# Two dense attentions with exponentials over three score banks, two score places and a ring of 15 units

## What is computed

```python
x = x + L0_attn(ln(x)); x = x + L0_ffn(ln(x))
x = x + L1_attn(ln(x)); x = x + L1_ffn(ln(x))
x = x + L2_attn(ln(x)); x = x + L2_ffn(ln(x))      # L2_attn: dense softmax attention + a sparse one
x = x + L3_attn(ln(x)); x = x + L3_ffn(ln(x))      # L3_attn: dense softmax attention
# the dense attention, 16 heads of 8 channels, 2048 tokens
scores = einsum('bhqd,bhkd->bhqk', q, k) * scale
out    = einsum('bhqk,bhkd->bhqd', softmax(scores), v)
```

## Time and profile before

| | us |
|---|---|
| median of 3 runs | 3074.58 (3073.29 to 3082.42) |
| the profiled execution, its own time | 3076.39 |
| its span, first to last instruction | 3074.5 |
| ACT in L1770, third layer / fourth layer | 495.7 / 496.0 |
| PE in L1729, third / fourth layer | 275.6 / 268.4 |
| PE in L1743, third / fourth layer | 274.2 / 268.4 |
| first dense attention, first half (in the trace) | 1486 to 1739 |
| first dense attention, second half | 1845 to 2109 |
| second dense attention | 2495 to 2998 |

### The profile page before, as it was taken

The page is one execution under the profiler, slowest core; times in us unless marked ns, Lnnn a source line. Parts: engine busy times, 40 slices in busy tenths (PEclk is TensorE's granted clock), DMA queues, the critical chain, the costliest instruction groups (busy, mean ns, idle before and its releaser), DMA issues. The chain is left out here.

```text
span 3074.5 us, 33207 instructions
## 1 busy us (share of the span) xinstructions
PE 2411.5 (78%) x12588; PEld 839.1 (27%) x12588; DVE 1912.1 (62%) x2779; ACT 1996.6 (65%) x1976; POOL 1072.1 (35%) x404
## 2 busy tenths in 40 slices
PE   3567777766757676765999889998669759999995
PEld 1122222244222222332222232223434412222223
DVE  5777988857999999866888527995330510111115
ACT  4789999912733333242899758997331259999991
POOL 4889999811099999431001200022000000000000
PEclk8888999979888888887999998999879879999998
DMA  2011112110154444102201200101010130111000
GB/s 72 1 42 42 42 56 69 42 52 8 28 171 159 163 161 157 52 13 64 43 13 35 40 0 2 20 3 43 7 39 0 44 53 14 35 29 22 14 6 27
DMA packets 66891, 144.63 MB, mean 47 GB/s; under 512 B 15592, under 2 KB 29889, under 8 KB 66018
## 3 DMA queue, kind: packets, MB, share of 16 engines
q1 hardware_dynamic: 66722, 142.40, 16.4%
HBM read 117.92 MB, written 24.25 MB: 46 GB/s over the span
## 5 line engine op out<-in xcount | busy, mean ns | idle before, releaser
L601 POOL TENSOR_TENSOR l0a_diff_pool<-l0a_A,l0a_a_of_t 128x2048 f32<-128x2048 f32 x128 | 532.5, 4203 | 36.2 <-ACT l0a_a_of_t L616 36.2
L1770 ACT ACTIVATE l2x_pT<-ps 128x1024 f32<-128x1024 f32 x512 | 495.7, 1021 | 17.9 <-PE ps L1729 16.0
L1770 ACT ACTIVATE l3he_pT<-ps 128x1024 f32<-128x1024 f32 x512 | 496.0, 1021 | 4.7 <-PE ps L1729 2.8
L1182 PE MATMUL ps<-l1s_hc,all_ident 128*128 128x512 f32 x512 | 287.7, 716 | 152.8 <-POOL l1s_hc L1153 100.6
L580 DVE SCALAR_TENSOR_TENSOR l0a_diff_dve<-l0a_A,l0a_pos,ps 128x512 f32<-128x512 f32 x512 | 344.9, 742 | 44.0 <-PE ps L455 44.0
L1144 POOL TENSOR_TENSOR l1s_dBx<-l1a_dtx,l1a_Bs 128x1024 f32<-128x1024 f32 x128 | 297.7, 2356 | 109.6 <-POOLq L878 109.6
L1168 ACT ACTIVATE ps<-l1a_dt,l1a_A 128x1024 f32<-128x1024 f32 x128 | 143.0, 1118 | 268.4 <-DVE l1s_hc L1227 216.1
L1729 PE MATMUL ps<-l3h_Qs,l3h_Ks 75*128 75x512 bf16 x1024 | 268.4, 385 | 33.0 <-DVE ps L1818 33.0
L1833 DVE COPY l3he_oT<-ps 128x512 f32<-128x512 f32 x16 | 11.1, 692 | 445.7 <-PE ps L1743 445.6
L1729 PE MATMUL ps<-l2m_Qs,l2m_Ks 75*128 75x512 bf16 x1024 | 275.6, 394 | 9.8 <-PEq L2052 9.8
L1743 PE MATMUL ps<-l2x_pT,l2m_Va 128*9 128x512 f32 x2048 | 274.2, 609 | 1.2 <-ACT l2x_pT L1770 1.2
(11 more groups left out here) (420 smaller groups left out, 3350.9 us busy)
## 6 DMA issues: line engine op xcount, KB each, us to landing
l1a_Bs<-l1a_bc SPq DMA_DIRECT2D x64, 512.0 KB, 3.6
l1s_Cs<-l1a_bc SPq DMA_DIRECT2D x64, 512.0 KB, 4.7
l0a_band_rows<-l0a_band SPq DMA_DIRECT2D x32, 512.0 KB, 5.4
l0a_band<-l0a_exps SPq DMA_DIRECT2D x16, 512.0 KB, 5.1
l2m_Ks<-l2m_parts SPq DMA_DIRECT2D x36, 128.0 KB
l2m_Qs<-l2m_parts SPq DMA_DIRECT2D x72, 64.0 KB
l3h_Ks<-l3h_parts SPq DMA_DIRECT2D x36, 128.0 KB
l3h_Qs<-l3h_parts SPq DMA_DIRECT2D x72, 64.0 KB
```

What stands on the lines that cost most here:

```text
L601: pool.tensor_tensor(out, window(s), atb[:, p % 2, :].unsqueeze(1).broadcast_to([P, 4, CH]), ALU.subtract).then_inc(diff_pool, 1)
L1182: mm = pe.matmul(g.ps[:, (4 + 2 * h + q) * CH:(5 + 2 * h + q) * CH], g.ident[:, :], hc[:, m % NHC, q * CH:(q + 1) * CH], start=(n == 0), s ...
L1770: act.activation(pT[:, turn % NPT, :], g.ps[:, slot * QC:(slot + 1) * QC], ACT.Exp).then_inc(expd, 1)
```

## The change

It alters the schedule of the two dense attentions and nothing else. The unit of the ring and of the accounting becomes the score block of 512 queries.

- **Exponentials over 1536 columns.** Units are taken three at a time, in triples; one ACT instruction reads three banks and writes three units. An attention of 1024 units has 342 of them instead of 512 (the last has one unit; each of the third layer's two halves of 512 units has 171, the last with two).
- **Two places of three banks** for the scores (`NST = 2`): triple `t` may be written when exponential `t - 2` is done.
- **A ring of 15 units** (`NPT = 15`) instead of 8 turns, which were 16 units; the place is the unit modulo 15.
- **Order on PE.** After each triple's scores at most one (n, c) of values is issued, if its last unit lies in triple `t - 2` or before; what is left at the end follows behind.
- **Waits on ACT.** Each triple waits for its scores, and for the values (of each half `c` that occurs) that read the units 15 earlier.
- SP's waits at a segment's end ask for the triple that holds the segment's last unit.

```diff
-NPT, NST = 8, 3
-ACC = NST * QC
+NPT, NST = 15, 2
+WIDE = 3 * CH
+ACC = NST * WIDE
...
+def triple_of(u, first):
+
+    done = 8 * TB * first
+    return -(-done // 3) + (u - done) // 3
...
 def head_values(pe, g, hd, pT, expd, accr, pvd, n, c, first):
...
-    if c == 0:
-        pe.wait_ge(expd, 4 * n + 4)
+    pe.wait_ge(expd, triple_of(8 * n + 6 + c, first) + 1)
...
 def head_segments(pe, g, hd, pT, sps, expd, accr, pvd, first, last):
 
+    due = [(n, c) for n in range(first * TB, last * TB) for c in range(2)]
+    for t, units in triples(first, last):
+        if t >= NST:
+            pe.wait_ge(expd, t - NST + 1)
+        for k, u in enumerate(units):
+            mm = head_scores(pe, g, hd, sps, u, (t % NST) * WIDE + k * CH)
+        mm.then_inc(sps, 1)
+        if due and triple_of(8 * due[0][0] + 6 + due[0][1], first) <= t - NST:
+            head_values(pe, g, hd, pT, expd, accr, pvd, *due.pop(0), first)
+    for n, c in due:
+        head_values(pe, g, hd, pT, expd, accr, pvd, n, c, first)
+
+
+def head_exps(act, g, pT, sps, expd, pvd, first, last):
+
+    for t, units in triples(first, last):
+        act.wait_ge(sps, t + 1)
         for c in range(2):
+            old = [(u - NPT) // 8 + 1 for u in units if u - NPT >= 8 * TB * first and (u - NPT) % 2 == c]
+            if old:
+                act.wait_ge(pvd[c], max(old))
+        at, src = ring_place(units[0], first), (t % NST) * WIDE
+        act.activation(pT[:, at:at + len(units), :], g.ps[:, src:src + len(units) * CH].rearrange("p (u t) -> p u t", t=CH), ACT.Exp).then_inc(expd, 1)
```

More of the change, by code:

```diff
@@ L1451 @@
 NQ = T // QC
-SEG = TB * 4
 NSEG = G4 * NQ
-NPT, NST = 8, 3
-ACC = NST * QC
+NPT, NST = 15, 2
+WIDE = 3 * CH
+ACC = NST * WIDE
 HB = TB // 2
@@ L1713, in head_prepare, with ring_place, exps_through, triples @@
     return hd
-def head_scores(pe, g, hd, pT, sps, expd, n, j):
+def triple_of(u, first):
+    done = 8 * TB * first
+    return -(-done // 3) + (u - done) // 3
+def ring_place(u, first):
+    return (u - 8 * TB * first) % NPT
+def exps_through(seg, first):
+    return triple_of(8 * TB * (seg + 1) - 1, first) + 1
+def triples(first, last):
+    units = range(8 * TB * first, 8 * TB * last)
+    return [(triple_of(units[k], first), units[k:k + 3]) for k in range(0, len(units), 3)]
+def head_scores(pe, g, hd, sps, u, at):
+    n, rest = divmod(u, 8)
+    j, c = divmod(rest, 2)
     seg, kt = divmod(n, TB)
     hg, qc = divmod(seg, NQ)
[L1720 to L1724, removed]
+    if kt == 0 and rest == 0:
         pe.wait_ge(hd.q_in[qc], hd.QIN * (hg + 1))
@@ L1727, in head_scores, with head_values @@
             pe.wait_ge(hd.k_in[hg % 2], hd.KIN * (hg // 2 + 1))
[L1728 to L1734, removed]
+    return pe.matmul(g.ps[:, at:at + CH], hd.Ks[:, hg % 2, j, kt * P:(kt + 1) * P], hd.Qs[:, qc, j, c * CH:(c + 1) * CH], start=True, stop=True)
+def head_values(pe, g, hd, pT, expd, accr, pvd, n, c, first):
     seg, kt = divmod(n, TB)
     hg = seg // NQ
-    if c == 0:
-        pe.wait_ge(expd, 4 * n + 4)
+    pe.wait_ge(expd, triple_of(8 * n + 6 + c, first) + 1)
     if kt == 0 and seg:
@@ L1743, in head_values @@
         mm = pe.matmul(g.ps[32 * j:32 * j + HS + 1, ACC + c * CH:ACC + (c + 1) * CH],
-                       hd.Va[:, kt, hg * 4 + j, :], pT[:, (4 * n + j) % NPT, c * CH:(c + 1) * CH],
+                       hd.Va[:, kt, hg * 4 + j, :], pT[:, ring_place(8 * n + 2 * j + c, first), :],
                        start=(kt == 0), stop=(kt == TB - 1))
@@ L1749, in head_segments @@
 def head_segments(pe, g, hd, pT, sps, expd, accr, pvd, first, last):
-    for j in range(4):
-        head_scores(pe, g, hd, pT, sps, expd, first * TB, j)
-    for n in range(first * TB, last * TB):
-        for c in range(2):
[L1755 to L1770, removed]
+    due = [(n, c) for n in range(first * TB, last * TB) for c in range(2)]
[12 more added lines that the diff above has]
+        act.wait_ge(sps, t + 1)
+        for c in range(2):
+            old = [(u - NPT) // 8 + 1 for u in units if u - NPT >= 8 * TB * first and (u - NPT) % 2 == c]
[3 more added lines that the diff above has]
+        act.activation(pT[:, at:at + len(units), :], g.ps[:, src:src + len(units) * CH].rearrange("p (u t) -> p u t", t=CH), ACT.Exp).then_inc(expd, 1)
 def head_attention(nc, g, tag, wqkv, bias, q_scale, k_scale, out_scale, OT):
@@ L1779, in head_attention @@
         r3 = Room(nc, ctx, tag + "e")
-        pT = r3.sb("pT", [P, NPT, QC])
+        pT = r3.sb("pT", [P, NPT, CH])
         oT = r3.sb("oT", [P, 2, QC])
@@ L1798, in _ @@
                     hg, qc = divmod(seg, NQ)
-                    sp.wait_ge(expd, (seg + 1) * SEG)
+                    sp.wait_ge(expd, exps_through(seg, 0))
                     hd.stack_next(sp, seg)
@@ L2146, in sums_out @@
                                 hg, qc = divmod(seg, NQ)
-                                sp.wait_ge(expd, (seg + 1) * SEG)
+                                sp.wait_ge(expd, exps_through(seg, first))
                                 if i < HSEG - 1:
```

## The result

The changed kernel takes 3179.9 us (median of 4 runs, 3178.2 to 3180.0) against 3073.9 before: ratio 1.036, 95% interval 1.033 to 1.038. The forecast was 3166, slower, range 3140 to 3205. The profiled execution took 3179.8 us with a span of 3177.9.

The account below looks back on a forecast made before the run. PE with its changes between scores and values was taken as the bound. Two new stalls, 1.08 us per 11.67 us cycle, gave 89.2 us, with small terms +91: 3167 us, 3166 as median; range 3140 to 3205.

Parts of the forecast that it names:

- PE was the bound, not ACT: Both attentions before: PE sets 1.945 us a pair, 0.25 us of it changing between scores and values; ACT 6% behind.
- Wide exponentials: ACT: 1536 columns take 1.45 us, 1.33 from start to start; some 12 us saved per attention, worth nothing alone.
- Ring: ACT: in triples 2 and 5 of eight, the values an exponential needs stand behind its own scores; 1.08 us a cycle.
- part 2: PE's order: eight triples a cycle, 11.67 us of PE work, values behind six of eight triples' scores, as many changes.
- First stall: PE before triple 4's scores: place free at v + 2.58 (v: values' start), PE ready at v + 1.64; 0.94 us.
- Second stall: PE, after triple 5: place free at v + 5.24 (v: values' start), PE ready at v + 5.10; 0.14 us.
- The sum: Loops at 2.4 GHz: 82.6 cycles of 1.08 us, 89.2 us; with 0.7 at 1.2 GHz and 1 for starts, +91 us.
- the upper bound: Loops: exponentials of 1.49 us without overlap, stalls 0.98 and 0.42, 1.40 us a cycle, 116 us, 3192 us in all.
- DVE, POOL, SP, tails: Other engines and the loops' ends: later than PE nowhere, tails keep two (n, c) of values; 0 us.
- ACT was the bound: Rival, both attentions: PE's gaps were waits for ACT, so 43 us saved in each, 2989 us; chance 0.03.
- The stall is covered: Rival, loops: values' signal comes early or the ring's wait is met earlier; 1.945 us a pair stays, 3077 us; chance 0.05.
- The clock falls: Rival, PE 92% busy in the loops: a fifth of the time at 1.2 GHz, 99 us more, 3265 us; chance 0.08.

Follow-up runs that it names:

- the first of the PE kernels: The kernel before, with each exponential handling only 128 of its 1024 columns once the ring is filled: 3062.9 us, ratio 0.998, fourth layer's loop 501.2 us.
- the bf16 kernels: Exponentials and V in bf16: kernel before 3260.7 us; plus 40 score matmuls per loop 3308.7; plus 12 fp32 matmuls instead 3292.1; changed kernel, 24-unit ring, 40 matmuls 3309.7.

## Why the prediction was right, and where it was off

- **PE was the bound, not ACT.** Shown: with a third of ACT's work the loop stayed at 501 us. The 0.25 us for changing to and fro came out as 0.22 when half the changes were taken away.
- **Wide exponentials.** 1.448 us and 1.33 to 1.35 from start to start, forecast 1.45 and 1.33. The page "ScalarE: Activation LUTs" of the Trainium skill, section "What ACT_TABLE_LOAD costs", gives 186 ns + 0.833 ns a column and an overlap of 93 ns, from which 1.47 and 1.37 were estimated; the trace is 1 to 3% below these estimates. By them the sum would have been about 10 us larger (0.02 in the first stall, 0.10 in the second), not the 8 that the prediction gives.
- **Ring.** The order of part 2 and the two triples that wait were as laid out: ACT waited for values 84 times in the fourth layer, forecast 86. The distances repeat after eight, 2.42 and 2.51 us before the two triples that wait, and one of 1.43 where about 1.6 was forecast, because ACT came 0.14 us later to it. With 18 units these waits were gone, and with them 48 of 61 us.
- **First stall.** Forecast release v + 2.58, measured 2704.50 - 2701.80 = v + 2.70, so 1.06 us instead of 0.94. **Second stall:** release forecast v + 5.24, measured 2712.36 - 2706.98 = v + 5.38, so 0.28 instead of 0.14. The term that was too small is the 0.04 us from values to ACT: 0.15 measured. It enters both stalls, 0.22 of the 0.30 us by which the cycle exceeds the forecast (13.05 against 12.75); the rest is hundredths, 1.35 for 1.33, 0.06 for 0.05, and PE's pieces, which add up to 11.70 for 11.67. I took the 0.04 from a wait that rides on its instruction; the new one didn't.
- **The sum.** With 1.38 us a cycle it is 82.6 x 1.38 = 114 us. The clock gave some back: 18 us less at 1.2 GHz in the second half, 3.5 and 4 us more in the other loops, each worth 1 - 1.945/3.64 = 0.47 us, so -5 us. That makes 109, and the loops grew by 109.9. Outside the loops the profiled execution was 6.5 us shorter (2056.9 to 2050.4), which I didn't trace; in the other kernels it was 2050 to 2060, leaving aside the one whose fp32 matmuls stand ahead of its loops. So the change's own cost is about 114 us, not the 91 forecast, and the clock and the rest took 11 us off what the profiled execution shows. The forecast came within 14 us by the luck of these 11. The 1.38 us a cycle are close to the 1.40 of the upper bound, but by another way: that bound had a slower exponential without overlap, and the exponential was as forecast.
- **DVE, POOL, SP, tails** at nothing: DVE only waits longer for PE (14 times in the fourth layer), and the loops account for the whole difference.
- **Rivals.** "ACT was the bound" fell with the first of the PE kernels. "The stall is covered" fell with the ring. "The clock falls" didn't happen here, at PE busy 92% with waits of 1.06 and 0.28 us in each 13: 1.00 in all three loops behind their starts. In the bf16 kernels it was 0.50 at PE busy 100%. So my evidence for and against it, the busy share, was the wrong measure, and the 0.08 was luck rather than judgement.

None of the kernels that do the whole work beats the one before beyond doubt; turns of two with the new accounting stand level with it.

## What to carry to other kernels

Before making instructions wider, look at starts, not at busy time: a wide instruction helps only if its engine is the one that never waits. When buffers are regrouped, lay each consumer's wait against the producer's written order: if what frees a place stands behind the work that needs the place, two engines run in series; three more units of ring took most of that away. And let the wait that comes last ride on the instruction itself: 0.06 us each time here, 0.09 where two waits stood in the separate one.

## What the runs showed of the hardware

- Changing on PE between bf16 scores over 75 rows and fp32 values in four column groups, and back, costs 0.22 us at 2.4 GHz (501.2 to 473.6 us with 128 changes fewer), 0.23 in the cycle with four changes instead of six (13.05 to 12.59 us), and about 0.25 by comparison of the two clocks. What in the change costs it wasn't taken apart.
- The granted clock didn't follow PE's busy record. Bf16 matmuls of 75 rows and 512 columns, back to back for 17.2 us, left 0.50; a loop of 600 us at PE busy 100% stayed at 0.50; 12 fp32 matmuls of 128 rows brought 1.00, and the loops with fp32 values held it, the changed one at PE busy 92%. "TensorE: Matmul & The Clock Gate" of the Trainium skill says in "What's actually happening" that "activity releases the throttle"; here activity by the busy record didn't, and rows, type and column groups weren't varied one at a time, so which of them counts stays open.
- With two semaphores to wait for, the wait written first rode on the exponential and the others went into an instruction of their own. When what that instruction waits for comes last, the exponential starts 0.12 us (one wait in it) or 0.15 us (two) after the values' records end, against 0.06 us when that wait rides on the exponential.
